# Four graph layers in one kernel: the gate and the small net of the next chunk move ahead of the norms in the equivariant layer, and 48 of its 100 slot scatters move into the message layer

## The chip, the cores and the metric

One NeuronCore of a Trainium2 chip runs the whole program. The metric is the time on the device in microseconds (us), the median of several executions. Engines are named as in the profile: PE (TensorE; its weight loads are PEld), DVE (VectorE), ACT (ScalarE), POOL (GpSimd), SP (SyncE, which here only issues DMAs).

## What is computed

Four graph layers over 50,000 nodes of 128 features and 12,500 edges (sorted by target), each followed by a residual and a layer norm:

```python
edge_index = jnp.stack([src, dst])
x = _layernorm(x + _L0_gnn_ref(x, edge_index, edge_attr_8, ...))       # attention over the edges
x = _layernorm(x + _L1_gnn_ref(x, edge_index, edge_type_16, ...))      # messages, mean over the edges, linear, own norm
x = _layernorm(x + _L2_gnn_ref(x, node_vec1, src, dst, edge_attr_4, edge_attr_8, ...))   # equivariant layer
x = _layernorm(x + _L3_gnn_ref(x, edge_index, ...))                    # two hypergraph convolutions with a batch norm
```

The equivariant layer, the one whose order changes, is in essence:

```python
h = silu(edge_scalars @ fc_w1/sqrt(8)) * SILU_NORM       # the "net" and the "gate"
w = h @ fc_w2/8                                          # w0..w3, the "weights"
s, v = linear maps of the source rows                    # the "features"
messages = products of w, s[src], v[src] and the edge's 4 attributes
out = segment_sum(messages, dst)/4 @ w_lin2              # "out", then the running sum over equal targets
```

## The kernel before

Only nodes that an edge names can change in an unusual way, so the kernel carries rows by edge and treats all other nodes by a closed formula (the dense part, class `Dense`). Its phases follow one another with a barrier between: index, attention, message, equivariant, tail. The edges go in 25 chunks (`NC`) of 500: 4 tiles (`CT`) of 125 edges (`TP`). Each engine has its own program of a loop over steps `s`; in one step it works on several chunks at different stages, for instance `turn(s + 1)` beside `norm(s - 3)`. Engines run their instructions strictly in the written order, and wait for one another by semaphores (`need(engine, semaphore, n)` waits until n chunks have passed that stage). So the order within a step is by hand.

**Message phase (L1294 to L1601).** POOL, per step: `fetch(s + 3)` gathers the source rows of a chunk with 4 indirect DMAs (tile `ms_ga`, 7 buffers), then `last_edges(s + 9)` looks up, with 4 more, the indices for a later chunk (`k_pq`; it ends at chunk 24, that is after step 15). PE, per step: `rows(s - 1)`, `turn(s + 2)` (4 transposes of the gathered rows, L1406), `message(s + 1)`, `update(s)`, and the moments of the dense part. ACT copies the turned rows (`source`, `ms_xs`), and behind that does `root`, `norm1(s - 2)` (`ms_n`) and `message(s + 1)`. DVE does the running sum over equal targets (`ms_S`, L1527), the residual, two sets of norm statistics, and `gained(s - 2)` (`ms_hg`, L1553), which waits for `norm1`.

**Equivariant phase (L1604 on).** POOL, per step: `fetch(s + 3)` (4 gathers into `eq_ga`, 7 buffers; the buffer must have been normed: `need(pool, s_y, c - RG + 1)`), then `payload(s - 5)`, 4 indirect DMAs that scatter 4 numbers of each edge into `table_S4` at the place `k_slot`; the last 5 chunks' payloads follow behind the loop. The table is read once, at the start of the tail. DVE, per step: `hidden(s + 1)` (`eq_hid`, the gate times the net), `scale(s - 3)` (`eq_rs`, `eq_nb`), `gated(s)` (6 products `eq_u`), `running(s - 1)` (`eq_S`), `residual(s - 2)` with 8 statistics, `aggregate(s - 2)` (`eq_mv`). At steps 2, 5, 9, 13 and 17 DVE also computes coefficients of the dense part (`dn.coefficients`, tiles `dg_...`), which take no part in the chunks. The orders of PE and ACT are in the listings below. `net` writes `eq_pH`, `gate` (Sigmoid) reads it; `hidden` reads both. `norm` is 8 ACT instructions (`eq_y`), `root` is the Sqrt (`eq_sd`). Sigmoid and Sqrt lie in different activation tables, so each step has two ACT_TABLE_LOADs.

Of the kernel before, what the change touches and what calls it, by code (L numbers as in the profile page):

```python
# [41 lines left out]
SILU = 1.6791767923989418  # L42
RING = 4
PQ = 6


class Chain:
# [464 lines left out]
def live(c):  # L512
    return 0 <= c < NC
# [373 lines left out]
def need(eng, sem, n):  # L887

    if not isinstance(n, int) or n > 0:
        eng.wait_ge(sem, n)  # L890
# [400 lines left out]
def message_phase(nc, g, K, T, dn, same):  # L1291

    with ExitStack() as ctx:
# [20 lines left out]
        dn.pS = a.ps("pS", [128, 512])  # L1314
        miss = a.sb("miss", [TP, CT])
        s_pq = [a.sem(f"last_edges{i}") for i in range(2)]
        s_idx, s_miss = a.sem("source_rows"), a.sem("miss")
        (s_w, s_eps, s_kind, s_tw, s_tA, s_xs, s_oneh, s_psM, s_m, s_S, s_psO,
         s_oF, s_psR, s_mean, s_h1, s_d1, s_d2, s_mv1, s_mv2, s_sd1, s_sd2, s_rs1, s_rs2, s_r1, s_r2, s_n1, s_hg, s_h2, s_y, s_twc, s_zero) = (
            a.sem(n) for n in ("weights", "eps", "kind", "typeW",  # L1320
# [50 lines left out]
        @block.gpsimd  # L1371
        def _(pool):
            nc.gpsimd.iota(kind[:], pattern=[[0, 1]], base=0, channel_multiplier=1).then_inc(s_kind, 1)
            pool.wait_ge(s_kind, 1)
            nc.gpsimd.tensor_copy(kindf[:], kind[:])
            nc.gpsimd.memset(eps[:], EPS).then_inc(s_eps, 1)
            pool.wait_ge(s_w, 16 * 7)

            def fetch(c):
                need(pool, s_h2, c - RG + 1)  # L1380
                need(pool, s_tA, c - RG + 1)
                need(pool, s_idx, c - PQ + 1)
                gathers(pool, s_ga[c % RG], K["idxS"], c, T["T1"], ga[c % RG])

            def last_edges(c):
                for t in range(CT * c, CT * c + CT):
                    nc.gpsimd.indirect_dma_start(out=K["pq"][:, t:t + 1], out_offset=None, in_=T["ptab"],  # L1387
                                                 in_offset=bass.IndirectOffsetOnAxis(ap=K["src"][:, t:t + 1], axis=0)).then_inc(s_pq[c % 2], 16)

            for s in range(-3, NC):  # L1390
                if live(s + 3):
                    fetch(s + 3)
                if live(s + 3 + PQ):
                    last_edges(s + 3 + PQ)

        @block.tensor
        def _(pe):
# [206 lines left out]
def equivariant_phase(nc, g, K, T, dn, same):  # L1604

    with ExitStack() as ctx:
        a = Place(nc, ctx, "eq")
        RG, RZ, LATE = 7, 4, 5
        A1, B1 = a.sb("A1", [D, D]), a.sb("B1", [D, D])
        fc1 = a.sb("fc1", [128, 64])  # L1610
        fA, fB, fC = (a.sb(n, [128, D]) for n in ("fA", "fB", "fC"))
# [65 lines left out]
        @block.gpsimd  # L1677
        def _(pool):
            nc.gpsimd.memset(eps[:], EPS).then_inc(s_eps, 1)

            def fetch(c):
                need(pool, s_y, c - RG + 1)
                gathers(pool, s_ga[c % RG], K["idxS"], c, T["T2"], ga[c % RG])

            def payload(c):
                for t in range(CT * c, CT * c + CT):
                    nc.gpsimd.indirect_dma_start(out=T["S4"], out_offset=bass.IndirectOffsetOnAxis(ap=K["slot"][:, t:t + 1], axis=0),  # L1687
                                                 in_=K["pay"][:, t, :], in_offset=None).then_inc(s_pay, 16)

            for s in range(-3, NC):  # L1690
                if live(s + 3):
                    fetch(s + 3)
                if live(s - LATE):
                    payload(s - LATE)
            for c in range(NC - LATE, NC):
                payload(c)
            pool.wait_ge(s_pay, 16 * NT)

        @block.tensor
        def _(pe):  # L1700
            pe.wait_ge(s_w, 16 * 9)

            def net(c):
                pe.wait_ge(s_ea8[c % 2], 16 * (c // 2 + 1))
                need(pe, s_hid, c)
                nc.tensor.matmul(pH[0:64, 0:CE], fc1[:], ea8[c % 2][:], start=True, stop=True).then_inc(s_psH, 1)

            def turn(c):
                have(pe, c)
                need(pe, s_sv, c)  # L1710
                for k in range(CT):
                    last = nc.tensor.transpose(pX[:, k * TP:(k + 1) * TP], ga[c % RG][:, k, :], K["ident"][0:TP, 0:TP])
                last.then_inc(s_tA, 1)

            def features(c):
                pe.wait_ge(s_xs, c + 1)
                nc.tensor.matmul(pX[:, 0:CE], A1[:], xs[:], start=True, stop=True)
                nc.tensor.matmul(pQ[:, 0:CE], B1[:], xs[:], start=True, stop=True).then_inc(s_psX, 1)

            def weights(c):  # L1720
                pe.wait_ge(s_hid, c + 1)
                need(pe, s_v, c)
                for w, p in ((fA, pA), (fB, pB), (fC, pC)):
                    last = nc.tensor.matmul(p[:, 0:CE], w[:], hid[:], start=True, stop=True)
                last.then_inc(s_psW, 1)

            def out(c):
                pe.wait_ge(s_u, c + 1)
                need(pe, s_S, c)
                nc.tensor.matmul(pO[:, 0:CE], oA[:], u2[:], start=True, stop=False)  # L1730
                nc.tensor.matmul(pO[:, 0:CE], oB[:], u4[:], start=False, stop=False)
                nc.tensor.matmul(pO[:, 0:CE], oC[:], u6[:], start=False, stop=True).then_inc(s_psO, 1)

            def rows(c):
                pe.wait_ge(s_S, c + 1)
                need(pe, s_z, c)
                for k in range(CT):
                    last = nc.tensor.transpose(pR[0:TP, k * D:(k + 1) * D], S[c % 2][:, k * TP:(k + 1) * TP], K["ident"][:])
                last.then_inc(s_psR, 1)

            for s in range(-2, NC + 2):
                if live(s - 2):
                    rows(s - 2)
                if live(s + 2):
                    net(s + 2)
                if live(s + 1):
                    turn(s + 1)
                    features(s + 1)
                    weights(s + 1)
                if live(s):  # L1750
                    out(s)

        @block.scalar
        def _(act):
# [7 lines left out]
            def source(c):  # L1762
                act.wait_ge(s_tA, c + 1)
                need(act, s_psX, c)
                nc.scalar.activation(xs[:], pX[:, 0:CE], ACT.Copy).then_inc(s_xs, 1)

            def features(c):
                i = c % 2
                act.wait_ge(s_psX, c + 1)
                need(act, s_u, c - 1)  # L1770
                nc.scalar.activation(sv[i][:], pX[:, 0:CE], ACT.Copy, scale=by_lin1)
                nc.scalar.activation(se[i][:], pQ[:, 0:CE], ACT.Copy, scale=by_lin1).then_inc(s_sv, 1)
# [15 lines left out]
            for s in range(-2, NC + 4):  # L1788
                if live(s + 1):
                    source(s + 1)  # L1790
                    features(s + 1)
                if live(s - 3):
                    norm(s - 3)
                if live(s + 2):
                    gate(s + 2)
                dn.roots(act, s)
                if live(s - 2):
                    root(s - 2)
# [590 lines left out]
```

## Time and profile before

| | us |
|---|---|
| median of 3 runs | 2579.2 (2573.97 to 2580.22) |
| the profiled execution | 2575.7 |
| its span, first to last instruction | 2573.9 |
| message phase in it, first gather to the next phase's first instruction | 699.4 to 1097.6 |
| equivariant phase, first gather to the last scatter's issue | 1098.4 to 1458.8 |

The profile is of one execution. Busy shares over the whole span are PE 55%, DVE 61%, ACT 33%, POOL 70%: none is the limit throughout, and the phases differ, so the views below are all cut to one of the two phases. "Idle before" in a row is the time for which the engine stood before that instruction, and behind the arrow stands who released it.

### The profile page before, as it was taken

Reading aid. Unit: us, or ns where it says so; the run is one execution under the profiler, and the core shown is the slowest. Engines: PE = TensorE matmul, PEld = TensorE weight load, DVE = VectorE, ACT = ScalarE, POOL = GpSimd, SP = SyncE. Lnnn points to the kernel's source line nnn. Section 1 sums busy time; section 2 is a strip of 40 time slices with the busy share of each in tenths; the row PEclk is TensorE's granted clock in tenths of the full one; section 3 lists DMA queues with packets and bytes.
Section 4 is the critical chain, followed back from the end, with each engine's and each line's share of the span. In section 5 each row is a group of like instructions: output and inputs, shape, how many; then the busy total and the mean of one; then the engine's idle time right before and its main releaser. Section 6 shows DMA issues by size and latency. Waiting matters only on the chain. (4 is left out here: it accounts for less than half of the span.)

```text
span 2573.9 us, 21863 instructions
## 1 busy us (share of the span) xinstructions
PE 1422.3 (55%) x4580; PEld 737.9 (29%) x4580; DVE 1568.6 (61%) x4901; ACT 861.3 (33%) x1813; POOL 1813.9 (70%) x1444
## 2 busy tenths in 40 slices
PE   6788488887456667267777367354454650011111
PEld 1344244444223333123333144222222430011110
DVE  8889277777538899857777544243344555434433
ACT  0111157776426677615665411111112330000000
POOL 5764777877188884055776778787875878877887
PEclk8899699999678888678898687777777875555555
DMA  1111344443345566244554476667797873323331
GB/s 24 26 33 36 80 119 130 124 128 84 84 96 129 138 153 157 64 109 98 123 123 112 77 198 191 151 183 177 183 170 198 224 205 94 84 63 72 75 71 43
DMA packets 358129, 297.95 MB, mean 116 GB/s; under 512 B 110941, under 2 KB 312428, under 8 KB 357981
## 3 DMA queue, kind: packets, MB, share of 16 engines
q1 hardware_dynamic: 260397, 225.43, 32.3%
q0 software_dynamic: 97600, 71.11, 14.2%
q8 instruction: 39, 0.64, 0.1%
q14 instruction: 93, 0.76, 0.1%
HBM read 199.75 MB, written 96.70 MB: 115 GB/s over the span
## 5 line engine op out<-in xcount | busy, mean ns | idle before, releaser
L2080 PE MATMUL tl_pX<-k_ident,tl_ga 125*128 125x125 f32 x400 | 85.4, 352 | 428.0 <-DMA tl_ga<-table_TE,k_s_idxE 326.3
L2191 DVE TENSOR_TENSOR_SCAN tl_S<-tl_same,tl_S,tl_pX 128x500 f32<-128x500 bf16 x96 | 120.3, 1253 | 317.3 <-PE tl_pX L2080 181.0
L479 POOL DMA_INDIRECT tl_ga<-table_TE,k_s_idxE x200 | 244.6, 1223 | 63.4 <-issue 59.1
L2080 PEld LDWEIGHTS tl_pX<-k_ident,tl_ga 125*128 125x128 f32 x400 | 58.1, 179 | 443.7 <-DMA tl_ga<-table_TE,k_s_idxE 336.4
L479 POOL DMA_INDIRECT eq_ga<-table_T,k_idxS x100 | 124.5, 1245 | 82.9 <-ACT eq_y L1785 53.8
L479 POOL DMA_INDIRECT at_ga<-x,k_src x100 | 139.6, 1396 | 43.4 <-issue 25.2
L479 POOL DMA_INDIRECT ms_ga<-table_T,k_idxS x100 | 135.5, 1355 | 47.0 <-issue 28.7
L1269 PE MATMUL tl_pCon<-dr_BC,dn_cT 128*128 128x512 f32 x196 | 132.9, 767 | 49.9 <-ACT dn_cT L1276 28.9
L479 POOL DMA_INDIRECT tl_ga<-table_TH,k_send x100 | 122.5, 1225 | 52.1 <-issue 51.8
L281 POOL DMA_INDIRECT table_ptab<-k_ef,ix_scatI x100 | 124.3, 1243 | 47.9 <-issue 47.9
L479 POOL DMA_INDIRECT at_gb<-xw,at_dstI x100 | 129.5, 1295 | 30.5 <-issue 30.5
L479 POOL DMA_INDIRECT tl_ga<-table_T,k_idxS x100 | 126.2, 1262 | 30.9 <-issue 30.9
L2031 POOL DMA_INDIRECT result<-tl_o,k_dst_end x100 | 121.3, 1213 | 36.4 <-issue 29.5
L1286 DVE TENSOR_TENSOR dr_o<-dr_x,tl_pMul 128x512 f32<-128x512 f32 x98 | 67.0, 684 | 127.8 <-PE tl_pMul L1270 91.7
L1687 POOL DMA_INDIRECT table_S<-k_pay,k_slot x100 | 123.2, 1232 | 30.5 <-issue 30.5
L2023 POOL DMA_INDIRECT tl_states<-table_T,k_s_idxS x100 | 122.0, 1220 | 30.5 <-issue 30.5
L2031 POOL DMA_INDIRECT result<-tl_o,k_src_end x100 | 121.0, 1210 | 30.5 <-issue 30.2
L2098 PE MATMUL tl_pR<-k_ident,tl_q 128*125 128x128 f32 x100 | 30.4, 458 | 178.3 <-ACT tl_q L2154 178.3
L1387 POOL DMA_INDIRECT k_pq<-table_ptab,k_src x76 | 111.6, 1469 | 23.2 <-issue 23.2
L1270 PE MATMUL tl_pMul<-dr_BM,dn_cT 128*128 128x512 f32 x196 | 124.9, 725 | 0.0
L2154 ACT ACTIVATE tl_q<-tl_h,k_cols 128x500 f32<-128x500 f32 x25 | 17.8, 712 | 286.7 <-DVE tl_h L2203 286.7
L461 PE MATMUL ix_pL<-ix_cur,ix_hiT 128*125 128x392 f32 x200 | 94.8, 557 | 22.1 <-DVE ix_junk L343 19.4
(464 smaller groups left out, 4358.3 us busy)
## 6 DMA issues: line engine op xcount, KB each, us to landing
dr_x<-x SPq DMA_DIRECT2D x97, 256.0 KB, 5.6
result<-dr_o SPq DMA_DIRECT2D x97, 256.0 KB, 3.8
dm_xT<-xT SPq DMA_DIRECT2D x32, 768.0 KB, 6.0
tl_fac<-table_dinv SPq DMA_DIRECT2D x50, 250.0 KB, 4.9
table_T<-at_y SPq DMA_DIRECT2D x50, 224.0 KB
table_T<-ms_y SPq DMA_DIRECT2D x50, 224.0 KB
table_T<-eq_y SPq DMA_DIRECT2D x50, 224.0 KB
table_TE<-tl_y SPq DMA_DIRECT2D x50, 224.0 KB
```

The costliest lines, as they stand in the source:

```text
L281: nc.gpsimd.indirect_dma_start(out=T["ptab"], out_offset=bass.IndirectOffsetOnAxis(ap=scatI[:, t:t + 1], axis=0), in_=K["ef"][:, t:t + 1], ...
L461: nc.tensor.matmul(pL[0:TP, t % 2, 0:LO], hiT[:, r % 2, k * TP:(k + 1) * TP], cur[:, r % 2, :], start=True, stop=True)
L479: nc.gpsimd.indirect_dma_start(out=buf[:, k, :], out_offset=None, in_=table, in_offset=bass.IndirectOffsetOnAxis(ap=index[:, CT * c + k:CT ...
L1269: nc.tensor.matmul(self.pC[b][:, 0:w], self.cT[:, h % 2, :], self.BC[:, i, 0:w], start=True, stop=True)
L1270: nc.tensor.matmul(self.pM[b][:, 0:w], self.cT[:, h % 2, :], self.BM[:, i, 0:w], start=True, stop=True).then_inc(self.s_mm, 1)
L1286: nc.vector.tensor_tensor(o, x, self.pM[b][:, 0:w], ALU.mult).then_inc(self.s_mul, 1)
L1387: nc.gpsimd.indirect_dma_start(out=K["pq"][:, t:t + 1], out_offset=None, in_=T["ptab"], in_offset=bass.IndirectOffsetOnAxis(ap=K["src"][:, ...
L1687: nc.gpsimd.indirect_dma_start(out=T["S4"], out_offset=bass.IndirectOffsetOnAxis(ap=K["slot"][:, t:t + 1], axis=0), in_=K["pay"][:, t, :], ...
L2023: nc.gpsimd.indirect_dma_start(out=states[:, k, :], out_offset=None, in_=T["T3"], in_offset=bass.IndirectOffsetOnAxis(ap=K["s_idxS"][:, k: ...
L2031: nc.gpsimd.indirect_dma_start(out=T["out"], out_offset=bass.IndirectOffsetOnAxis(ap=index[:, CT * c + k:CT * c + k + 1], axis=0), in_=o[i ...
L2080: last = nc.tensor.transpose(pX[j % 2][:, k * TP:(k + 1) * TP], ga[j % RG][:, k, :], K["ident"][0:TP, 0:TP])
L2191: nc.vector.tensor_tensor_scan(S[i][:], same[j % RM][:], pX[i][:, 0:CE], 0.0 if j % NC == 0 else S[1 - i][:, CE - 1:CE], ALU.mult, ALU.add ...
```

## The change

Three edits. (1) In the equivariant phase ACT does `gate(s + 2)` right behind `source(s + 1)`, ahead of `features(s + 1)` and `norm(s - 3)`; before, it came behind the norm. (2) There PE does `turn(s + 1)` ahead of `net(s + 2)`; before, behind it. (3) The scatters of the first 12 chunks (48 of 100) are issued in the message phase, four of them behind `last_edges` in each even step from 2 to 24; the other 52 stay in the equivariant phase, four behind `fetch` in each even step from 0 to 24, and none is left behind the loop. The count, the sizes and the arithmetic of all instructions stay.

```diff
+SLOTS = 12
@@ message_phase, gpsimd
+            def records(c):
+                need(pool, s_idx, c - PQ + 1)
+                for t in range(CT * c, CT * c + CT):
+                    nc.gpsimd.indirect_dma_start(out=T["S4"], out_offset=bass.IndirectOffsetOnAxis(ap=K["slot"][:, t:t + 1], axis=0),
+                                                 in_=K["pay"][:, t, :], in_offset=None).then_inc(s_rec, 16)
+
             for s in range(-3, NC):
                 if live(s + 3):
                     fetch(s + 3)
                 if live(s + 3 + PQ):
                     last_edges(s + 3 + PQ)
+                if s > 0 and s % 2 == 0 and s // 2 <= SLOTS:
+                    records(s // 2 - 1)
+            pool.wait_ge(s_rec, 64 * SLOTS)
@@ equivariant_phase, gpsimd
-                if live(s - LATE):
-                    payload(s - LATE)
-            for c in range(NC - LATE, NC):
-                payload(c)
-            pool.wait_ge(s_pay, 16 * NT)
+                if s >= 0 and s % 2 == 0 and SLOTS + s // 2 < NC:
+                    payload(SLOTS + s // 2)
+            pool.wait_ge(s_pay, 64 * (NC - SLOTS))
@@ tensor
+                if live(s + 1):
+                    turn(s + 1)
                 if live(s + 2):
                     net(s + 2)
                 if live(s + 1):
-                    turn(s + 1)
                     features(s + 1)
                     weights(s + 1)
@@ scalar
                 if live(s + 1):
                     source(s + 1)
+                if live(s + 2):
+                    gate(s + 2)
+                if live(s + 1):
                     features(s + 1)
                 if live(s - 3):
                     norm(s - 3)
-                if live(s + 2):
-                    gate(s + 2)
```

PE in one step of the equivariant phase, before (`eq_pR` rows, `eq_pH` net, `eq_pX<-k_ident` turn, then features, weights and out):

```order
L1738 MATMUL eq_pR<-k_ident,eq_S0 125x128 x4
L1706 MATMUL eq_pH<-eq_ea80,eq_fc1 64x500
L1712 MATMUL eq_pX<-k_ident,eq_ga4 128x125 x4
L1717 MATMUL eq_pX<-eq_xs,eq_A1 128x500
L1718 MATMUL eq_pQ<-eq_xs,eq_B1 128x500
```

and after:

```order
L1746 MATMUL eq_pR<-k_ident,eq_S0 125x128 x4
L1720 MATMUL eq_pX<-k_ident,eq_ga4 128x125 x4
L1714 MATMUL eq_pH<-eq_ea80,eq_fc1 64x500
L1725 MATMUL eq_pX<-eq_xs,eq_A1 128x500
L1726 MATMUL eq_pQ<-eq_xs,eq_B1 128x500
```

The transposes changed places with the net; the net now stands between the transposes and the matmuls that need ACT's copy of them.

ACT in one step of the equivariant phase, before (`eq_xs` source, `eq_sv` and `eq_se` features, `eq_y` norm, `eq_sg` gate, `eq_sd` root):

```order
L1765 ACTIVATE eq_xs<-eq_pX 128x500
L1771 ACTIVATE eq_sv1<-eq_pX 128x500
L1772 ACTIVATE eq_se1<-eq_pQ 128x500
L1785 ACTIVATE eq_y1<-eq_z3,eq_nb1,eq_rs1 125x128 x4
L1785 ACTIVATE eq_y1<-eq_ga0,eq_nb1,eq_rs1 125x128 x4
L1760 ACT_TABLE_LOAD
L1760 ACTIVATE eq_sg<-eq_pH 64x500
L1777 ACT_TABLE_LOAD
L1777 ACTIVATE eq_sd0<-eq_mv0,eq_eps 125x8
```

and after:

```order
L1774 ACTIVATE eq_xs<-eq_pX 128x500
L1769 ACT_TABLE_LOAD
L1769 ACTIVATE eq_sg<-eq_pH 64x500
L1780 ACTIVATE eq_sv1<-eq_pX 128x500
L1781 ACTIVATE eq_se1<-eq_pQ 128x500
L1794 ACTIVATE eq_y1<-eq_z3,eq_nb1,eq_rs1 125x128 x4
L1794 ACTIVATE eq_y1<-eq_ga0,eq_nb1,eq_rs1 125x128 x4
L1786 ACT_TABLE_LOAD
L1786 ACTIVATE eq_sd0<-eq_mv0,eq_eps 125x8
```

The gate with its table load moved from behind the norm to in front of the features; both loads are still there.

POOL in the middle of the message phase, before (`ms_ga` fetch, `k_pq` last edges):

```order
L1387 DMA k_pq<-table_ptab,k_src 125x1 x4
L479 DMA ms_ga6<-table_T1,k_idxS 125x128 x4
L1387 DMA k_pq<-table_ptab,k_src 125x1 x4
L479 DMA ms_ga0<-table_T1,k_idxS 125x128 x4
L1387 DMA k_pq<-table_ptab,k_src 125x1 x4
```

and after:

```order
L1388 DMA k_pq<-table_ptab,k_src 125x1 x4
L1394 DMA table_S4<-k_pay,k_slot 12500x4 x4
L480 DMA ms_ga6<-table_T1,k_idxS 125x128 x4
L1388 DMA k_pq<-table_ptab,k_src 125x1 x4
L480 DMA ms_ga0<-table_T1,k_idxS 125x128 x4
L1388 DMA k_pq<-table_ptab,k_src 125x1 x4
L1394 DMA table_S4<-k_pay,k_slot 12500x4 x4
```

In every second step four scatters now stand between POOL's look-ups and its next gathers.

## Rows read from the trace of the kernel before

**Rows 1.** Waits view, 697 to 1091 us: who waited for whom, us, times, longest.
```profile
PE ms_pA L1406 <- DMA ms_ga<-table_T,k_idxS: 62.5, 13, 12.4
...
POOL ms_ga L479 <- DVE ms_h L1561: 11.2, 3, 6.0
```
**Rows 2.** Timeline (start, length), message phase: gather, turn and sum, chunks 2 and 9.
```profile
728.73 1.21 POOL L479 DMA_INDIRECT ms_ga<-table_T,k_idxS  x1 [0.30 <-issue]
...
732.11 1.10 PE L1406 MATMUL ms_pA<-k_ident,ms_ga 125*128 125x125 f32 x4 [8.16 <-DMA ms_ga<-table_T,k_idxS]
...
823.52 1.21 POOL L479 DMA_INDIRECT ms_ga<-table_T,k_idxS  x1 [0.30 <-issue]
...
830.39 1.10 PE L1406 MATMUL ms_pA<-k_ident,ms_ga 125*128 125x125 f32 x4 [5.28 <-DMA ms_ga<-table_T,k_idxS]
...
842.19 1.24 DVE L1527 TENSOR_TENSOR_SCAN ms_S<-dst_same,ms_S,ms_m 128x500 f32<-128x500 bf16 x1
```
**Rows 3.** Timeline, message phase, the same for chunk 19.
```profile
962.96 1.21 POOL L479 DMA_INDIRECT ms_ga<-table_T,k_idxS  x1 [0.31 <-issue]
...
969.28 0.59 PE L1406 MATMUL ms_pA<-k_ident,ms_ga 125*128 125x125 f32 x4
...
980.57 1.24 DVE L1527 TENSOR_TENSOR_SCAN ms_S<-dst_same,ms_S,ms_m 128x500 f32<-128x500 bf16 x1
```
**Rows 4.** Windows view, message phase: window, length, busy per engine (count), clock, DMA.
```profile
700.00:964.00 264.00, 160.44 (x410) 78.10 (x411) 192.47 (x734) 147.29 (x329) 216.76 (x156) 0.80 0.54 134
...
980.70:1056.60 75.90, 52.66 (x136) 25.78 (x136) 72.59 (x276) 55.06 (x133) 16.12 (x11) 0.79 0.50 132
```
**Rows 5.** Tile view of table_S: the scatters (ns min/median/max, first and last start).
```profile
L1687 POOL DMA_INDIRECT table_S<-k_pay,k_slot x100: 1182/1190/2222, 1181.4 to 1457.6; - x100
```
**Rows 6.** Waits view, 1095 to 1462 us, equivariant phase.
```profile
POOL eq_ga L479 <- ACT eq_y L1785: 53.8, 6, 23.4
```
**Rows 7.** Tile view of eq_xs, the copy at the head of each chunk.
```profile
L1765 ACT ACTIVATE eq_xs<-eq_pX x25: 566/587/588, 1112.0 to 1424.6; 128x500 f32<-128x500 f32 x25
```
**Rows 8.** Timeline, one step of the equivariant phase at full clock.
```profile
1277.45 0.58 ACT L1760 ACTIVATE eq_sg<-eq_pH 64x500 f32<-64x500 f32 x1
...
1278.88 1.02 PE L1706 MATMUL eq_pH<-eq_ea,eq_fc 128*64 128x500 f32 x2 [1.44 <-DVE eq_hid L1811]
...
1279.84 0.65 PE L1712 MATMUL eq_pX<-k_ident,eq_ga 125*128 125x125 f32 x4
...
1280.19 0.20 DVE L1857 RECIPROCAL eq_rs<-eq_sd 125x8 f32<-125x8 f32 x1 [1.45 <-ACT eq_sd L1777]
...
1281.16 1.10 PE L1717 MATMUL eq_pX<-eq_xs,eq_A 128*128 128x500 f32 x2 [0.68 <-ACT eq_xs L1765]
...
1283.14 0.59 ACT L1771 ACTIVATE eq_sv<-eq_pX 128x500 f32<-128x500 f32 x1 [2.03 <-PE eq_pQ L1718]
...
1287.29 1.28 ACT L1760 ACT_TABLE_LOAD   x1
...
1287.84 0.64 DVE L492 BATCH_NORM_AGGREGATE eq_mv<-eq_st 125x2 f32<-125x6 f32 x8
...
1288.58 0.58 ACT L1760 ACTIVATE eq_sg<-eq_pH 64x500 f32<-64x500 f32 x1
```
**Rows 9.** Timeline of PE's weight loads: features begin, and rows begin 16 matmuls later.
```profile
1292.29 0.30 PEld L1717 LDWEIGHTS eq_pX<-eq_xs,eq_A 128*128 128x128 f32 x2 [0.91 <-ACT eq_xs L1765]
...
1298.68 0.19 PEld L1738 LDWEIGHTS eq_pR<-k_ident,eq_S 128*125 128x125 f32 x1 [0.23 <-issue]
```
**Rows 10.** Windows view, the five coefficient stretches of DVE and their sum.
```profile
1186.80:1199.80 13.00, 0.71 (x5) 0.41 (x3) 12.79 (x17) 2.87 (x4) 10.87 (x8) 0.68 0.33 80
...
sum 41.40, PE 6.95 PEld 3.55 DVE 40.59 ACT 13.28 POOL 28.04; mean PE 1.39 PEld 0.71 DVE 8.12 ACT 2.66 POOL 5.61
```
**Rows 11.** Windows view, ten us behind the third of these stretches.
```profile
1253.00:1263.00 10.00, 8.79 (x13) 3.50 (x14) 8.34 (x27) 2.71 (x7) 7.27 (x6) 0.50 0.40 74
```
**Rows 12.** Timeline, the last chunk's norm in the equivariant phase.
```profile
1454.68 1.63 ACT L1785 ACTIVATE eq_y<-eq_ga,eq_nb,eq_rs 125x128 f32<-125x128 f32 x4
```

More of the change, by code:

```diff
@@ L1316, in message_phase @@
         s_pq = [a.sem(f"last_edges{i}") for i in range(2)]
-        s_idx, s_miss = a.sem("source_rows"), a.sem("miss")
+        s_idx, s_miss, s_rec = a.sem("source_rows"), a.sem("miss"), a.sem("records")
         (s_w, s_eps, s_kind, s_tw, s_tA, s_xs, s_oneh, s_psM, s_m, s_S, s_psO,
@@ L1607, in equivariant_phase @@
         a = Place(nc, ctx, "eq")
-        RG, RZ, LATE = 7, 4, 5
+        RG, RZ = 7, 4
         A1, B1 = a.sb("A1", [D, D]), a.sb("B1", [D, D])
```

## Prediction

> **What bounds the kernel now.** I read the waits of each phase first, then single steps in the timeline, then windows. *Message phase:* PE waits for gathered rows (62.5 us in 13 waits; its weight loads show as much again), while POOL waits for compute in 3 places only, 11.2 us [rows 1]. Up to 964 us POOL never stands: 156 DMAs, 216.8 us busy, and 0.30 us of issue before each make 263.6 of 264 us [rows 2, 4]. That is 8 DMAs, 12.1 us at the shortest (1.21 + 0.30), measured as 13.8 us per chunk (chunk 2's last gather at 728.7 us, chunk 19's at 963.0 [rows 2, 3]). From a chunk's last gather the rest follows in lockstep: PE turns 6.9 us later for chunk 9 and 6.3 us later for chunk 19, and the running sum of the chunk before starts 11.8 and 11.3 us behind the turn [rows 2, 3], since ACT copies the turned rows ahead of the norm for which DVE's gain waits. So POOL sets the pace until chunk 19. Then DVE does: 72.6 of 75.9 us busy [rows 4].
>
> *Equivariant phase:* here POOL waits for ACT, 53.8 us [rows 6], and the pace is a ring of 11.13 us from gate to gate [rows 8]: gate to net 1.43 (DVE's hidden between), net to turn 0.96, turn to features 1.32 (ACT's copy between), features to ACT's copies 1.98, copies and norm 4.15, table load 1.29 to the next gate; together 11.13. The norm and two engines' handovers lie in a ring in which the net of the next chunk needn't be. Between first and last copy there are 24 intervals in 312.6 us [rows 7]. POOL and the chunks end together: the last norm at 1456.3 us [rows 12], the last scatter's issue at 1458.8 [rows 5].
>
> **The change part by part.** The profiled execution took 2575.7 us, 3.5 below the median of 2579.2; the sum is made against the first and carried over to the median.
>
> *Gate and net moved.* The old ring opens: the gate no longer stands behind the norm, and the net fills PE while ACT copies. What is late next is the busiest engine. PE: features to rows 6.39 [rows 9], rows about 0.9 (four transposes like the turn's 0.65, with one more load shown ahead), turn 0.65, net 0.96 [rows 8], together 8.9. DVE: scale to the end of the aggregates 8.3 [rows 8], hidden 0.6, together 8.9. ACT: copies and norm 4.15, two loads 2.56, gate 0.58, copy 0.59, root 0.3, together 8.2. All three are nearly full and hand over to one another in each step (DVE's hidden, PE's net and features, ACT's norm and root, DVE's scale), so I take 9.2 us and keep 8.9 and 10.2 as ends; the upper one is the case that about 1 us of handovers stays open. Three of the 24 intervals have no norm yet and gain nothing that counts. 21 x (11.13 - 9.2) = **-40.5 us** (-20 to -47). The head gains some 2 us, since the first turn no longer waits behind two nets.
>
> *What of it is given back.* DVE's dense coefficients take 41.4 us in five stretches in which PE does almost nothing (0.71 of 13 us) [rows 10]. Before, they cost that and little more: 312.6 - 41.4 - 21 x 11.13 leaves 37.5 us, about 28 of it the three first intervals, so some 9 us for everything else, the slow clock included. PE's granted clock behind the third stretch is 0.50 for 10 us, the lower of its two levels, 1.2 GHz; PE had stood before it [rows 11]. In the old ring only net, turn and features (4.3 us) feel that; in the new one PE's whole step does, so PE loses up to 5 us each time, partly in DVE's shadow. I take 2 us more than before for each of the five, +10, less 4 for lesser dips elsewhere that a fuller PE may spare: **+6** (0 to +15). Sum for the phase: **-36 us** (-18 to -49).
>
> *POOL in that phase.* This is what the scatters' move pays for: 8 DMAs per step are 12.1 us, more than the new 9.2. With 52 scatters left it is 152 DMAs at 1.51 to 1.54 = 230 to 234 us, 6 per step or 9.2 us, in a phase of about 325. A gather may run 7 chunks ahead of its norm and its turn comes three steps behind that release, some 27 us, against 6 to 12 us of issue and about 7 to land; so it stays hidden, without much to spare. The scatters were hidden before too: moving them gains nothing by itself. The phase's tail is compute in both kernels; 8 scatters instead of 36 stand behind the last gather.
>
> *The scatters in the message phase.* They stand before gathers on the engine that sets the pace. Steps 2, 4, ... 14 put 7 x 4 = 28 of them ahead of chunk 19's gathers, each 1.19 busy [rows 5] + 0.30 = 1.49: 41.7 us. Chunk 19 has 2.9 us to spare: its turn came 6.3 us behind the last gather, and 3.4 us is what the shortest landings take (728.73 to 732.11 for chunk 2 [rows 2]). So its turn is late by 39. Behind it POOL has no look-ups left and issues 4 to 8 DMAs per step, 6 to 12 us against DVE's 13, and the gathers of chunks 20 to 24 would be late by 48 to 60 us against the old issue times but are needed 39 us later too and had the more in hand the further back they stand (POOL even waited for DVE there [rows 1]), so they arrive as they are needed. DVE was 96% busy from chunk 18's sum on [rows 4] and can't catch up. **+39 us** (34 to 46). The upper end comes from the price: POOL's DMAs cost 216.8/156 = 1.39 busy here against 1.21 at the shortest, which for 28 more would be 47 us; I take the lower one because these stretches seem to come with DVE's work, of which there is no more than before. Issue, wait at the end and the new semaphore cost nothing: POOL is done tens of us before the phase ends.
>
> [...]
>
> **Sum:** 2575.7 + 39 - 36 = 2578.7, and on the median 2579.2 + 3 = **2582 us**. Two large terms cancel.
>
> **The rivals.** *A, cancel (forecast):* 2582, own range 2571.5 to 2587, which is also what a measurement of this kernel can't tell from no change (0.3% is 7.7 us). *B, faster:* the message phase isn't POOL's but DVE's. For it: DVE needs 75.9/6 = 12.65 us per chunk when POOL is out of the way, little under POOL's 13.8 [rows 4], and chunk 19's turn waited for no gather [rows 3]. Where DVE sets a step's end, a scatter costs nothing; with half of them so, the term is some +20: +20 - 36, 2563. Against: POOL's stretch without one wait, which leaves no time to fill. A ring of 8.9 us with the clock kept gives the same side: +39 - 49 = 2569. *C, slower:* the new ring stays at 10.2 us or more. Its place is PE's net: it now waits for hidden of the chunk before and holds features, weights and out behind it, so a late DVE stops PE, which then falls to the slow clock, late features hold ACT's norm and root, and DVE's scale waits for the root. At 10.2 us per step 21 x 0.93 = 19.5, with the 2 of the head and less 6, leaves 15.5: +23.5, 2603. It decides from 9.45 us on: 21 x 1.68 = 35.3 gives 31.3, and 39 - 31.3 is 7.7. For it: no engine has more than 1 us of slack per step. Against: every one of those links lies a step ahead. *D, slower:* each scatter costs 1.7 us in the message phase: 47.6 - 2.9 = +45, with landings up to 3 us later, +48 - 36, 2591. *E, it doesn't do what it says:* the gate was not what held the ring, and the step stays at 11.1; 2579.2 + 39 = 2618. The ring's members add up to the step to within 0.01 us, so I hold this to be unlikely.
>
> **Chances.** A 0.45, B 0.22, C 0.17, D 0.12, E 0.04. So faster 0.22, same 0.45, slower 0.33. The range for 8 in 10 takes in B's and D's times and C's: 2563 to 2603, with E and the far ends outside.
>
> **What would show it.** In the message phase: the turn of chunk 19 at 1008 (969 before), POOL without a wait until about 1057, PE's wait for gathers up by tens of us (62.5 before), the next phase's first gather at 1137 (1098). In the equivariant phase: intervals between the copies `eq_xs` of 9.2 in quiet stretches, 312.6 in all down to about 278, POOL's wait for the norm under 53.8 but not gone, the gate right behind the copy. Wrong would be: chunk 19 turned before 1000 (B), quiet intervals over 9.5 (C), PE waiting for `eq_ga` in the equivariant phase (POOL too slow there), or scatters of more than 1.4 us in the message phase (D).

## The result: 0.5% faster, where no change was forecast

The changed kernel took **2564.0 us** (median of 4 runs, 2561.7 to 2568.9), the kernel before 2576.9 beside it: a ratio of 0.9952, 95% interval 0.9931 to 0.9974. The forecast was 2582 and "no change"; the time lies at the lower edge of the range of 2563 to 2603. The profiled execution of the changed kernel spans 2567.1 us, that of before 2573.9. So the sums below account for the 6.8 us between the two profiled executions; the medians are 12.8 us apart. Most of what lies between is that the profiled execution of the changed kernel was the slowest of its four (2568.9).

I cut both traces at the first gather of three phases. Tile views of the gathers of the changed kernel (ns min/median/max, first and last start in us), message, equivariant and last phase:

```profile
L480 POOL DMA_INDIRECT ms_ga<-table_T,k_idxS x100: 1208/1213/2398, 699.7 to 1064.8; - x100
...
L480 POOL DMA_INDIRECT eq_ga<-table_T,k_idxS x100: 1208/1213/2273, 1144.6 to 1406.9; - x100
...
L480 POOL DMA_INDIRECT tl_ga<-table_T,k_idxS x100: 1208/1212/6190, 1455.7 to 1610.8; - x100
```

The same three of the kernel before:

```profile
L479 POOL DMA_INDIRECT ms_ga<-table_T,k_idxS x100: 1206/1212/2391, 699.4 to 1008.9; - x100
...
L479 POOL DMA_INDIRECT eq_ga<-table_T,k_idxS x100: 1206/1212/1680, 1098.4 to 1402.8; - x100
...
L479 POOL DMA_INDIRECT tl_ga<-table_T,k_idxS x100: 1206/1210/6197, 1466.5 to 1621.6; - x100
```

| us, first gather to first gather | before | after | difference | forecast |
|---|---|---|---|---|
| message phase | 399.1 | 445.0 | +46 | +39 |
| equivariant phase | 368.1 | 311.1 | -57 | -36 |
| from the last phase's first gather to the end | 1107.4 | 1111.4 | +4 | 0 |

What follows the last phase's first gather is the same code on the same data; in the other ten kernels below it took 1102.5 to 1109.5 us, so the 4 us are scatter between executions. (Ahead of the message phase lie 699.4 and 699.7 us.) Two terms of opposite sign, as forecast, and both larger. The +46 is of one pair of executions: the experiments hold three more kernels with this message code, 441.6 to 443.1 us, and five more with that of before or with the scatters behind its last gather, 399.2 to 401.4. By the means, 443.0 against 399.9, the term is +43.

**Message phase.** Waits view of the changed kernel, 697 to 1140 us (us, times, longest):

```profile
PE ms_pA L1416 <- DMA ms_ga<-table_T,k_idxS: 112.1, 15, 12.9
```

PE waits 112.1 us for gathered rows where it waited 62.5 [rows 1]. Timeline, changed kernel: the first and the last gather of chunk 19 and its turn:

```profile
1004.67 1.21 POOL L480 DMA_INDIRECT ms_ga<-table_T,k_idxS  x1 [0.30 <-issue]
...
1009.22 1.27 POOL L480 DMA_INDIRECT ms_ga<-table_T,k_idxS  x1 [0.31 <-issue]
...
1015.72 0.59 PE L1416 MATMUL ms_pA<-k_ident,ms_ga 125*128 125x125 f32 x4
```

The turn is at 1015.7 (969.3 before [rows 3]), 6.5 us behind the last gather as against 6.3. From the first gather of chunk 19 to the next phase it is 140 us in both kernels (1144.6 - 1004.7; before, 1098.4 - 958.4). So the loss arises ahead of chunk 19. Windows view of the changed kernel (window, length, busy and count per engine, clock, DMA share, GB/s), up to chunk 19 and the stretch behind it:

```profile
700.00:1004.60 304.60, 155.70 (x402) 75.88 (x402) 189.02 (x720) 140.80 (x314) 249.77 (x180) 0.74 0.49 116
1023.70:1101.30 77.60, 48.10 (x137) 23.42 (x136) 75.18 (x285) 58.88 (x140) 47.37 (x33) 0.84 0.54 130
```

POOL: 180 DMAs, 249.8 us busy, and 180 x 0.30 of issue make 303.8 of 304.6 us; it never stands. Further on DVE is 97% busy (75.2 of 77.6), the counterpart of the 96% in [rows 4].

**Equivariant phase.** Tile view, changed kernel, the copy at the head of each chunk and the two groups of scatters:

```profile
L1774 ACT ACTIVATE eq_xs<-eq_pX x25: 563/587/592, 1153.9 to 1417.8; 128x500 f32<-128x500 f32 x25
...
L1697 POOL DMA_INDIRECT table_S<-k_pay,k_slot x52: 1186/1198/2640, 1169.3 to 1419.0; - x52
L1394 POOL DMA_INDIRECT table_S<-k_pay,k_slot x48: 1186/1222/2415, 777.2 to 1078.4; - x48
```

First to last copy: 263.9 us, against 312.6 [rows 7]. Timeline, one step of the changed kernel, to be read beside [rows 8]:

```profile
1308.53 0.64 DVE L1821 SCALAR_TENSOR_TENSOR eq_hid<-eq_pH,eq_sg 64x500 f32<-64x500 f32 x1
...
1308.79 0.59 PE L1720 MATMUL eq_pX<-k_ident,eq_ga 125*128 125x125 f32 x4
...
1309.31 1.05 PE L1714 MATMUL eq_pH<-eq_ea,eq_fc 128*64 128x500 f32 x2
...
1309.42 0.59 ACT L1774 ACTIVATE eq_xs<-eq_pX 128x500 f32<-128x500 f32 x1 [0.47 <-issue]
...
1310.29 1.10 PE L1725 MATMUL eq_pX<-eq_xs,eq_A 128*128 128x500 f32 x2
...
1311.32 0.58 ACT L1769 ACTIVATE eq_sg<-eq_pH 64x500 f32<-64x500 f32 x1
...
1312.27 0.59 ACT L1780 ACTIVATE eq_sv<-eq_pX 128x500 f32<-128x500 f32 x1 [0.38 <-issue]
```

The net (1309.3) runs while ACT copies (1309.4), the features follow without a wait, and the gate (1311.3) stands ahead of ACT's copies of them: the ring of before is open. The next copy is at 1318.17, 8.75 us behind this one.

### The profile page after: what moved, and what is told of

It is laid out like the page before. It is cut to its first block and busy times, and to the rows that moved or that the text cites. A ratio compares the mean times of both kernels' runs of the same rounds, so it can differ in the third digit from the quotient of the medians.

```text
span 2567.1 us, 21864 instructions
## 1 busy us (share of the span) xinstructions
PE 1396.4 (54%) x4580; PEld 726.2 (28%) x4580; DVE 1565.7 (61%) x4901; ACT 861.6 (34%) x1813; POOL 1825.5 (71%) x1444
## 3 DMA queue, kind: packets, MB, share of 16 engines
q0 software_dynamic: 97600, 71.11, 14.5%
## 5 line engine op out<-in xcount | busy, mean ns | idle before, releaser
L480 POOL DMA_INDIRECT at_ga<-x,k_src x100 | 139.5, 1395 | 43.4 <-issue 25.2
L480 POOL DMA_INDIRECT ms_ga<-table_T,k_idxS x100 | 143.3, 1433 | 36.4 <-issue 30.2
L282 POOL DMA_INDIRECT table_ptab<-k_ef,ix_scatI x100 | 124.2, 1242 | 48.8 <-issue 48.8
L2041 POOL DMA_INDIRECT result<-tl_o,k_dst_end x100 | 120.6, 1206 | 37.5 <-issue 29.5
L2041 POOL DMA_INDIRECT result<-tl_o,k_src_end x100 | 120.4, 1204 | 30.5 <-issue 30.2
L1388 POOL DMA_INDIRECT k_pq<-table_ptab,k_src x76 | 100.2, 1318 | 23.2 <-issue 23.2
L500 DVE TENSOR_SCALAR tl_o<-tl_z,tl_mv,tl_rs 125x128 f32<-125x128 f32 x200 | 60.2, 427 | 58.4 <-DMA result<-tl_o,k_dst_end 57.1
```

The costliest lines, as they stand in the source:

```text
L282: nc.gpsimd.indirect_dma_start(out=T["ptab"], out_offset=bass.IndirectOffsetOnAxis(ap=scatI[:, t:t + 1], axis=0), in_=K["ef"][:, t:t + 1], ...
L480: nc.gpsimd.indirect_dma_start(out=buf[:, k, :], out_offset=None, in_=table, in_offset=bass.IndirectOffsetOnAxis(ap=index[:, CT * c + k:CT ...
L500: last = nc.vector.tensor_scalar(out[:, r, :], z[:, r, :], mv[:, r, 0:1], rs[:, r:r + 1], ALU.subtract, ALU.mult)
L2041: nc.gpsimd.indirect_dma_start(out=T["out"], out_offset=bass.IndirectOffsetOnAxis(ap=index[:, CT * c + k:CT * c + k + 1], axis=0), in_=o[i ...
```

## The experiments

| kernel | time, us | ratio to before (95%) | message | equivariant |
|---|---|---|---|---|
| changed kernel | 2564.0 | 0.9952 (0.9931 to 0.9974) | 445.0 | 311.1 |
| e1 new order, no scatter moved | 2548.5 | 0.9913 (0.9900 to 0.9927) | 401.4 | 343.1 |
| e2 scatters moved, old order | 2611.0 | 1.0168 (1.0149 to 1.0187) | 442.5 | 361.8 |
| e3 ACT's gate alone | 2583.6 | 1.0053 (1.0038 to 1.0069) | 441.6 | 337.0 |
| e4 PE's turn alone | 2586.8 | 1.0057 (1.0036 to 1.0077) | 443.1 | 334.9 |
| e5 records behind the last gather | 2516.5 | 0.9796 (0.9778 to 0.9813) | 399.2 | 311.7 |
| e6 half of them there | 2536.6 | 0.9849 (0.9834 to 0.9864) | 419.4 | 309.9 |
| e7 = e5, coefficients behind the loop | 2505.1 | 0.9731 (0.9718 to 0.9744) | 400.9 | 298.7 |
| e8 = before, coefficients behind the loop | 2567.3 | 0.9971 (0.9951 to 0.9991) | 399.4 | 358.7 |
| e9 = e1, scatters spread from the first step | 2534.4 | 0.9832 (0.9813 to 0.9851) | 399.3 | 328.6 |
| e10 = e7, 52 records in place of 48 | 2518.0 | 0.9764 (0.9745 to 0.9784) | 406.1 | 301.8 |

Phases are cut as above, in the one profiled execution of each kernel. The first four, e1, e2, e5 and e3, ran together, then e4, e6, e7 and e8, then the last two; each group has its own runs of before in its ratios, so I compare ratios across groups.

### e1: is POOL really the bound once the order is new?

```
 kernel before, with only these two edits
 TensorE:  rows(s-2); turn(s+1); net(s+2); features(s+1); weights(s+1); out(s)
 ScalarE:  source(s+1); gate(s+2); features(s+1); norm(s-3); root(s-2)
```

> The kernel before with the new order on TensorE and ScalarE only; all 100 record scatters stay in the equivariant phase. Theory of the prediction (GpSimd's eight DMAs a step, 12.1 us, would set the step): source copies 12.1 us apart in quiet steps, message phase as before (399 us), time 2577 or little under. Rival (GpSimd has a lead of several chunks: 200 DMAs are 306 us of work, and the phase after the change lasts 311): most of the 57 us is there without moving a scatter: first gather to the next phase's first gather 311 to 330 us, time 2520 to 2540, and GpSimd's wait for the norm (53.8 us before) falls below 15 us.

In between. 2548.5 us: the order alone is worth more without the scatters' move than with it. Tile view of e1:

```profile
L1766 ACT ACTIVATE eq_xs<-eq_pX x25: 564/587/588, 1112.1 to 1388.8; 128x500 f32<-128x500 f32 x25
...
L1687 POOL DMA_INDIRECT table_S<-k_pay,k_slot x100: 1182/1187/1574, 1176.3 to 1437.3; - x100
```

Waits of e1's POOL, 1102 to 1440 us:

```profile
POOL table_S L1687 <- issue: 30.5, 100, 0.3
POOL eq_ga L479 <- issue: 30.0, 97, 0.7
POOL eq_ga L479 <- ACT eq_y L1786: 26.1, 3, 15.4
```

Up to chunk 17 the quiet steps are 8.8 to 9.5 us with 8 DMAs a step on POOL, since gathers run ahead; then mostly 11.7, POOL's pace, and the last scatters stand behind the last gather, so that 56.6 us pass from the last copy to the next phase (37.9 in the changed kernel). POOL stood 26.1 us, all of it before 1204 us, and then worked until 1437. So "8 DMAs per step are 12.1 us, more than the new 9.2" is true of a step, but the phase is bounded by the sum: 200 DMAs and their issue, 311 us here (250.3 busy and the 60.5 of issue above), plus the 26 us for which POOL stands.

### e2: the scatters' move alone

```
 changed kernel; TensorE's and ScalarE's order as before
```

> The changed kernel with the old order on TensorE and ScalarE: only the 48 record scatters move to the message phase. Theory: message phase +46 us as in the changed kernel, quiet steps of the equivariant phase still 11.1 us, that phase 368 us less at most 8 (head and end, where GpSimd has fewer DMAs): time 2615 to 2623. Rival (the scatters themselves held up the equivariant phase, through GpSimd or the DMA queue): that phase 15 us or more shorter, time 2608 or less. Second rival (the message phase's loss comes with the new order in some way): message phase less than +40 us.

The theory held in the phases: 442.5 us (+43) in the message phase, and the copies of the equivariant phase still 311.1 us apart in all, first to last. That phase is 6 us shorter, 4.7 of them behind the last copy (37.2 against 41.9): fewer scatters stand behind the last gather. The prediction had put this end at nothing. The time, 2611.0, is 4 us under the expected 2615 to 2623; the kernel before took 2570.1 beside it, 7 less than the 2576.9 that the range was built on.

### e5: the same 48 scatters behind the last gather

```diff
-                if s > 0 and s % 2 == 0 and s // 2 <= SLOTS:
-                    records(s // 2 - 1)
+            for c in range(SLOTS):
+                records(c)
```

> The changed kernel, but the 48 record scatters of the message phase are issued behind its last gather and last edge fetch, where GpSimd stood idle for 87 us before. Theory (the +46 us come from gathers delayed in GpSimd's order, nothing else): message phase back at 399 us (48 x 1.5 = 72 us fit into 87), equivariant phase 311 us, time 2515 to 2525. Rival (the scatters slow the other engines or the DMA queue wherever they stand): message phase +10 us or more though no gather is late, time 2530 or more.

The theory held in all its numbers. Tile views of e5, the gathers of both phases and the 48 scatters:

```profile
L480 POOL DMA_INDIRECT ms_ga<-table_T,k_idxS x100: 1205/1210/2387, 698.2 to 1006.7; - x100
...
L480 POOL DMA_INDIRECT eq_ga<-table_T,k_idxS x100: 1205/1212/1702, 1097.5 to 1360.4; - x100
...
L1394 POOL DMA_INDIRECT table_S<-k_pay,k_slot x48: 1182/1187/2414, 1008.2 to 1091.3; - x48
```

The same scatters that cost 43 to 46 us among the gathers cost nothing behind them: POOL had nothing to do from 1009 to 1098 us in the kernel before. The gain of the order stays whole, 311.7 us, and the kernel is 2.0% faster than before.

### e6: how much does each scatter cost?

```diff
-                if s > 0 and s % 2 == 0 and s // 2 <= SLOTS:
-                    records(s // 2 - 1)
+                if s > 0 and s % 4 == 0 and s // 4 <= SLOTS // 2:
+                    records(s // 4 - 1)
+            for c in range(SLOTS // 2, SLOTS):
+                records(c)
```

> The changed kernel with 24 of the 48 record scatters among the message phase's gathers (4 at every fourth step, so 12 of them ahead of chunk 19's gathers in place of 28) and 24 behind the last gather. Theory (each scatter ahead of chunk 19 costs its 1.45 us and the 0.3 us behind it, once 2.9 us of slack are used): message phase 12 x 1.75 - 2.9 = +18 us against 399, equivariant phase 311, time 2530 to 2538. Rival (all scatters ahead of the last gather count, 24 x 1.75 = 42): message phase +35 or more. Second rival (each costs the 1.49 us of the undisturbed ones): +15.

+20.3 us (419.4 - 399.1), near the theory's 18 and far from the rival's 35, and chunk 19's first gather comes 20.5 us later than before, counted from the phase's first. So only those ahead of chunk 19 count, but no slack is taken off: the phase is late by as much as the gather, here and in the changed kernel (45.9 and 46.0). A scatter costs 20.5 / 12 = 1.71 us here, 46.0 / 28 = 1.64 in the changed kernel. These prices carry the scatter of single executions: with 28 scatters ahead of it that gather comes 302.0 to 305.0 us behind the first one (four kernels, mean 303.1), with none 258.4 to 261.3 (seven kernels, mean 259.7), which is 43.4 / 28 = 1.55 each.

### e3 and e4: one edit each

```
 e3: ScalarE as changed, TensorE's net ahead of turn as before
 e4: TensorE as changed, ScalarE's gate behind norm as before
```

> The changed kernel with TensorE's order of before: only ScalarE's gate stands ahead of the features, scatters as after the change. Theory (one ring through both engines, each move opens a part of it): quiet steps about 10.0 us, between 8.95 (both) and 11.13 (none), equivariant phase 325 to 335 us, time 2577 to 2590. Rival (the gate alone opens the ring, TensorE's order is of no weight): quiet steps 8.9 to 9.1, time 2564 to 2568.

> The changed kernel with ScalarE's order of before: only TensorE's turn stands ahead of net, scatters as after the change. The run with ScalarE's gate alone gave quiet steps of 9.6 us and 11.5 to 12.5 us behind the coefficient stretches, phase 337.0 us. Theory (one ring, each move opens a part of it; TensorE's order is what makes the step insensitive to the slow clock): quiet steps about 10.2 us, steps behind the stretches under 1 us longer than those, phase 328 to 336 us, time 2575 to 2585. Rival (the gate is the whole of it): quiet steps 11.1 us, phase 362 us, time 2605 to 2612.

One ring, opened in parts, as the theory had it, the gate's part somewhat larger than expected (9.65, not 10.0): quiet steps of 11.1 us with none, 9.65 with the gate, 10.1 with the turn, 8.9 with both. e4's time, 2586.8, lies 2 us over its range. The two differ behind a coefficient stretch: e3's next step is 11.5 to 12.5 us long, about 2 us over its quiet ones, e4's 10.2 to 11.4, mostly 0.5 over, and once 1.2, where under 1 was expected. So it is TensorE's order that takes away most of the price of the slow clock. Against e2, which has neither and the scatters in the same places, the gate alone is worth 25 us, the turn alone 27, both together 51.

### e7 and e8: the coefficient stretches taken out of the loop

```diff
-                dn.coefficients(dve, s)
+            for s in range(NC):
+                dn.coefficients(dve, s)
```

and ScalarE's roots of them likewise; e7 on top of e5, e8 on top of the kernel before.

> The kernel with the records behind the last gather (2516.5 us), with VectorE's coefficient pieces and ScalarE's roots of them moved out of the equivariant loop, behind its last chunk. Theory (the coefficient pieces do not lie beside anything: what they cost in the loop, 264.2 - 24 x 8.9 = 50 us, is paid behind it as well, where 41.4 us of VectorE's work and four round trips to ScalarE stand): all steps 8.8 to 9.0 us, no slow clock after the start, source copies 213 to 218 us from first to last, end of the phase 38 + 40 to 50 us, time 2508 to 2522. Rival (the loop slows on its own from time to time, through the clock or the queue): steps over 9.5 us remain without the pieces.

> The kernel before with the coefficient pieces and their roots moved behind the loop in the same way; order and scatters as before. Theory (the steps of 12.9 us behind each piece come from TensorE's slow clock after its pause, and the old order is sensitive to it): all steps from the fifth on 11.1 us, none of 12.8, source copies 312.6 -> 258 to 263 us, time 2560 to 2575. Rival (the long steps come from the scatters or another cause in that loop): steps of 12.7 us and over remain.

In e7 the copies run from 1114.7 to 1331.6, 217.0 us for 24 steps, 17 of them of 8.8 to 8.9 us. The stretches cost 47.2 us in the loop (264.2 - 217.0) and 34.4 behind it (72.4 - 38.0 from the last copy to the next phase), less than their 41.4 us of work, and less than the 40 to 50 expected: some of it probably lies beside the last norms now. Not all steps came down: seven are 9.1 to 10.7 us long, the first of them the phase's own first, and two of these are over the 9.5 us that the rival had named. The clock is full in all of them (view below). That is the fastest kernel of this study, 2505.1 us.

In e8 my theory fell, though the time is within its range. The copies are 272.6 us apart, not 258 to 263. Steps of 12.7 to 12.8 us remain, eight of them, every second step from 1195 us on, though no stretch is left. Windows view of e8:

```profile
1219.20:1222.20 3.00, 2.82 (x4) 1.33 (x5) 2.97 (x6) 0.13 (x1) 2.63 (x2) 0.50 0.42 94
1222.50:1243.00 20.50, 16.50 (x49) 7.45 (x47) 14.12 (x50) 16.14 (x30) 16.25 (x14) 1.00 0.60 138
1243.10:1246.10 3.00, 2.87 (x4) 1.38 (x5) 2.97 (x6) 0.08 (x1) 2.39 (x3) 0.50 0.33 89
1246.40:1266.90 20.50, 16.48 (x49) 7.45 (x47) 14.13 (x50) 16.17 (x30) 16.25 (x14) 1.00 0.60 140
```

The third column from the right is PE's granted clock. With PE busy 16.5 of 20.5 us in the old order, the clock falls to its lower level of 1.2 GHz for at least the 3 us of these windows in every second step, and that step is 1.6 us longer. The same view of e7, whose loop has the new order:

```profile
1130.00:1339.20 209.20, 205.99 (x600) 94.53 (x599) 193.79 (x596) 174.07 (x321) 167.97 (x136) 1.00 0.68 162
```

PE is busy 206 of 209 us and the clock is full throughout. So the old order lost time to a clock that fell with no stretch in the loop. What made it fall no run varies by itself.

### e9 and e10: is POOL's work the floor?

```diff
 e9, on e1
-                if live(s - LATE):
-                    payload(s - LATE)
-            for c in range(NC - LATE, NC):
-                payload(c)
+                if live(s):
+                    payload(s)
```

```diff
 e10, on e7
-SLOTS = 12
+SLOTS = 13
```

> The kernel with the new order alone (2548.5 us), all 100 record scatters still in the equivariant phase, but four at each of its 25 steps from the first on, where before they began five steps later and 20 stood in a row behind the last step. With the new order alone GpSimd had 200 DMAs in 343 us and stood still only three times, 26.1 us in all, in the first 95 us. Theory (GpSimd's 316 us of DMAs are the floor of that phase once TensorE's and ScalarE's order is new; the standstill at the start is what a better order can win): phase 322 to 335 us, time 2528 to 2542. Rival (the late scatters set only the end, and the steps go by gathers: putting scatters ahead of early gathers makes the steps 12 us from the start): phase 340 us or more, time 2546 or more. Second rival (the floor is not GpSimd): phase near 311, time 2516 to 2522.

> The kernel with the records behind the last gather and the coefficient pieces behind the loop (2505.1 us), with 52 record scatters in the message phase in place of 48. In it seven steps of the equivariant phase were 9.1 to 10.7 us. Theory (those steps wait for GpSimd, which is close to its limit there; 52 x 1.69 = 88 us still fit behind the last gather, where 91 us are free): message phase 399 to 401 us, those steps under 9.1, time 2499 to 2505. Rival (the message phase ends on the scatters now): message phase 403 us or more, time 2505 to 2512.

e9: the theory held. POOL waited for no norm, and the phase is 328.6 us, 14.5 shorter than e1's. So even with not one scatter moved out of the phase the order is worth 1.7%. The phase is still 16.9 us longer than e5's: POOL's 200 DMAs with their issue take 312 us without a stand, from the first gather at 1100.3 to 1412.7 (the 316 us of the expectation were too many).

e10: the rival held in the phase, 406.1 us, and the time, 2518.0, is over even its 2512. By the ratios e10 is 8.5 us slower than e7; the phases give 5.2 and 3.1 of it. The last of the 52 scatters starts at 1098.2 us and the next phase begins 5.6 us later, as in e7, where 48 had filled the free time already (1100.0 and 5.4); from the phase's first gather the last scatter starts 5 us later than in e7, and the phase is 5 us longer. My 91 us of free time had left out what stands between the last scatter and the next phase. Nor did the long steps go (10.0, 11.3 and 10.5 us among the last ones), though PE's waits for gathered rows behind 1133 us are only 3.0 us there and 1.9 in e7. What makes those steps long beyond these waits is open.

## Why the prediction was wrong, point by point

**What bounds each phase: right.** POOL to chunk 19, then DVE; the equivariant phase by the ring. The turn of chunk 19 was forecast at 1008 and came at 1015.7, POOL worked without a wait to 1066 (1057 forecast), the next phase began at 1144.6 (1137).

**Message term, +39 put, +46 measured: two mis-sized parts.** *The price of a scatter:* I took 1.49 us. Up to chunk 19's gather 28 more DMAs came with 45.7 us more of POOL's time (busy 212.8 to 250.1 us, and 28 x 0.30), 1.63 each, and 1.55 by the means in e6. I had this end in hand (1.39 busy as the phase's mean) and argued it away, since the stretched DMAs "seem to come with DVE's work, of which there is no more than before". In this pair they became more: 19 of 152 were over 2 us before, 26 of 180 after; over all kernels it is 19 to 22 of 152 against 21 to 26 of 180. *The slack of 2.9 us:* I read it as the difference between this chunk's gather-to-turn time and the shortest. That distance is 6.3 us before and 6.5 after, but 4.6 to 6.3 in the other kernels with no scatter ahead and 3.7 in e6, and the phases of e6 and of the changed kernel are late by the whole delay of the gather. By the means the miss is some 4 us, 1.7 of price and 2.9 of slack; the other 3 of the 46 are within the scatter of executions. Rival D's +45 came near through two errors that cancel: a price of 1.7, over the 1.63 of this pair, and the same slack taken off.

**Where the long DMAs come from.** Timeline of the changed kernel, one of them and what DVE did meanwhile:

```profile
783.92 2.38 POOL L480 DMA_INDIRECT ms_ga<-table_T,k_idxS  x1 [0.30 <-issue]
784.02 1.24 DVE L1537 TENSOR_TENSOR_SCAN ms_S<-dst_same,ms_S,ms_m 128x500 f32<-128x500 bf16 x1
...
785.50 0.67 DVE L1543 TENSOR_TENSOR ms_mean<-ms_S,ms_deg 128x500 f32<-128x500 f32 x1
```

In the trace of the changed kernel 32 DMAs from 700 to 1065 us are over 2 us, 2.24 in the mean, and 2.08 us of that lies under a TENSOR_TENSOR or the scan of DVE; the 168 under 1.3 us have 0.24 us of TENSOR_TENSOR and hardly any scan beside them. By the Trainium skill (SBUF — State Buffer, "Who interferes with whom") a DVE instruction with two SBUF inputs contends with a GpSimd instruction that reads SBUF, because its second input comes through the read interface that the two share. The same section tells of a probe in which `tensor_tensor` did not stall DMA. The trace agrees with the first in which DMAs are long, 2.2 to 2.4 us for 1.2, and with the second it doesn't fit: of the 22 DMAs that DVE's L1571 (TENSOR_TENSOR on `ms_h`, both inputs in SBUF) overlaps by more than 0.25 us, 11 are over 2 us; beside L1552 (`ms_xu`, one input in PSUM) none of 20 is over 1.32. But lying beside is not enough: of the 21 beside L1563 (`ms_hg`, both inputs in SBUF) only 2 are over 2 us. No run takes those inputs away, so this is a correlation and not shown.

**Gate and net, -40.5 put.** The step came to 8.95 us, not 9.2: it is what PE and DVE sum up to (8.9 each), and the 0.3 us I added for handovers were not needed. That is 4 to 5 us. The head gained 4.2 us, not 2 (from the first gather to the first copy 13.5, then 9.3; e2 keeps the 13.5, so it is the order).

**What is given back, +6 put: the step that failed.** Its size and its sign were wrong. The copies are 48.8 us closer together; 21 x (11.13 - 8.97) is 45.4 of it, so what I had put at +6 came out at -3.4. In intervals between the 25 copies:

| | before | after |
|---|---|---|
| 5 with a coefficient stretch in them | 93.4 us | 92.7 |
| 7 of 12.8 to 12.9 us, where the clock is slow | 89.9 | none |
| the other quiet ones | 8 x 11.1, last 11.9 | 16 x 9.0 |
| the first three | 28.4 | 27.6 |

The five with a stretch gained nothing; there the ring's gain is given back in full (5 x 2.2 = 11 us). But I had booked the slow clock as a new cost of the new order, +10. It was a cost of the old one: 7 steps of 1.7 us, 12 us, which it spares. Five of the seven stand right behind a stretch, the other two do not. The forecast took 37.5 us as about 28 for the three first intervals and "some 9 us for everything else, the slow clock included"; in the table these 9 are the 12 of the slow steps and 0.7 of the last, less 3.7, since the five intervals with a stretch are that much shorter than 41.4 and five rings. And from "In the old ring only net, turn and features (4.3 us) feel that" it concluded that the new ring must feel it more. The windows show the reverse. Before, around the third stretch: the slow clock, then the step behind the stretch:

```profile
1249.80:1263.30 13.50, 9.09 (x14) 3.66 (x15) 11.37 (x33) 3.01 (x7) 9.86 (x8) 0.50 0.36 69
1256.50:1269.40 12.90, 12.02 (x26) 5.27 (x26) 6.40 (x24) 8.17 (x16) 7.87 (x7) 0.74 0.48 103
```

After, the same places:

```profile
1276.90:1283.70 6.80, 2.90 (x4) 0.87 (x5) 6.56 (x14) 1.86 (x2) 5.58 (x5) 0.53 0.27 59
...
1291.20:1300.20 9.00, 9.00 (x27) 4.11 (x28) 8.49 (x27) 8.55 (x16) 5.19 (x5) 1.00 0.70 186
```

The timeline shows where PE takes up work again behind its stand, first before, then after:

```profile
1253.54 1.90 PE L1706 MATMUL eq_pH<-eq_ea,eq_fc 128*64 128x500 f32 x2 [6.76 <-DVE eq_hid L1811]
```

```profile
1280.80 1.90 PE L1714 MATMUL eq_pH<-eq_ea,eq_fc 128*64 128x500 f32 x2 [6.60 <-DVE eq_hid L1821]
```

PE stands as long in both (6.8 and 6.6 us, for the same hidden). In the new order the turn and ACT's copy are already done, so net, features, weights and out follow back to back, and the clock is full again 3 us later, inside the interval; in the old one PE goes on by pieces and stays slow for 10 us more, into the next step. Runs e3 and e4 place this in TensorE's order: the step behind a stretch is about 2 us longer with the old one and mostly 0.5 us with the new. Why the slow clock lasts longer there I infer from PE's gaps; no run varies these alone.

**"The phase's tail is compute in both": wrong, 4 us.** From the last copy to the next phase 41.9 us became 37.9; e2 has 37.2 with the old order, so the scatters behind the last gather held it.

**"This is what the scatters' move pays for": half right.** Without it POOL binds (e1, 343.1 us, 32 over the changed kernel's 311.1), so "moving them gains nothing by itself" holds but for the 6 us of e2. But their place was what cost: among the gathers they cost 43 to 46 us to win 32 (and only 17 against e9, which spreads them in their own phase), and rows read for the prediction [rows 4], with 11 DMAs in 75.9 us behind chunk 18's sum, showed POOL's free time behind the gathers. The forecast had no rival in which the change is good and its place is bad.

**The sum.** Of rivals, B's condition "A ring of 8.9 us with the clock kept" came true together with a message term like D's: +45 - 49 = -4, where the two phases gave -11. The other 8 us of the -57 are the tail (4), the head (2) and the old order's slow steps less what the stretches gave back (12 - 11), with 1 left to rounding. I had priced B and D as alternatives; they were independent of each other.

## What to carry to other kernels

Where an engine's queue sets the pace in one stage and stands idle in the next, moved work belongs behind the last thing that others wait for: here 48 DMAs cost 43 to 46 us or nothing by their place in the queue alone. Bound a queue by the sum over the phase and the lead it may build, not by the work of one step; e1 and e9 have the same DMAs and differ only in where the scatters stand, 14.5 us. And when a ring is opened, look for what the old one cost beyond its step: long steps in a trace that stand behind no visible cause (12.8 among 11.1 us) are a term of the sum.

## What the hardware showed that I had not expected

In a loop in which PE was busy 16.5 of 20.5 us, with short stands in every step, the granted clock fell to its lower level again and again, for at least 3 us in every second step (e8); in one with 206 of 209 us busy it never fell (e7). One stand of 6.6 to 6.8 us cost 7 us of slow clock when dense work followed and 13.5 when it did not. In the message phase of the changed kernel an indirect DMA's issue on GpSimd took 1.19 us at its shortest and up to 2.4, and the long ones lay beside DVE's two-input operations, without each such operation making one long.
